# Rotary sum of queries and keys formed in PSUM by accumulated transposes instead of by an addition on VectorE

## The chip, the cores and the metric

The kernel runs on one core of a Trainium2 chip. The metric is the device time of one execution in microseconds (us); a median of several executions is compared with the median of the changed kernel. All data are fp32.

## What is computed

The input x is 4 sequences of 256 tokens with 256 features. One decoder block is applied: gated linear attention with decay, then four experts chosen by token id, then a second short attention whose sequence axis is the batch; a layer norm follows each. Only the first part is touched by the change:

```python
q = silu((x @ Wq).reshape(b, n, 16, 16)); k = silu((x @ Wk).reshape(b, n, 16, 16))
v = (x @ Wv).reshape(b, n, 16, 16)
q, k = rotate(q), rotate(k)      # concat(x1*cos - x2*sin, x1*sin + x2*cos) per head
# chunks of 128 tokens, two for a sequence:
scores = einsum('bthd,bshd->bhts', qi, ki) * D
o = einsum('bhts,bshd->bthd', scores, vi) + einsum('bthd,bhde->bthe', qi * decay_q, S)
S = lam_C * S + einsum('bshd,bshe->bhde', ki * decay_k, vi)
x = layernorm(x + groupnorm(o * sigmoid(x @ Wg1 @ Wg2)) @ Wo)
```

The rotation of a tile is a sum of two products: the tile times a cosine table, and the tile with the halves of each head swapped times a sine table.

## The kernel before

The 1024 tokens are 8 tiles of 128. The program is written by hand for each engine (TensorE, VectorE, ScalarE, GpSimd, and SyncE for the transfers); semaphores alone order the engines, and each engine runs its own list strictly in order. Attention runs in rounds: round i works on tile i in its first steps and on tiles i-1 and i-2 in its later ones. From round 7 on the rounds of the experts and of the last part are woven in; the change doesn't touch these.

TensorE's list in round i (`attention_round` in its block): `transpose_qk(i)`, four transposes of 128x128, the two of q into bank 2 and then the two of k into bank 7; `attend(i-1)` (state or scores times values); in even rounds `make_state(i/2)`, k times v for the state that the second chunk of the sequence needs, into bank 7; `proj_qkv(i+1)`; `scores(i, g)` for four groups g of four heads, in banks 3 and 4 by turns, of which group g waits until VectorE has emptied group g-2; `transpose_on(i-2)`, `turn_back(i-1)` and `project_o(i-2)`. In round 7 `transpose_h(0)` comes before the scores. In round 0 `transpose_experts` stands behind the transposes.

VectorE's list: `copy_kT(i)`; `gate_o(i-2)` and `norm_o(i-2)` (two wide operations, one reduction and a chain of eleven small ones, lines 681 to 686); in even rounds `decay_state`, two scalings of bank 7; `ln_apply`; `rope_cos(i+1)`, the cosine product for the next tile; the masks of scores 0 and 1, `rope_add(i+1)`, the masks of scores 2 and 3 (`mask_scores`, line 717); `residual1(i-2)`, which waits for `project_o`, and the statistics of the layer norm. Rounds 3 and 5 also prepare weights here.

ScalarE: `expand_q(i)` (eight copies of 32 partitions from bank 2), `silu_qk(i+1)`, which makes `qk`, `copy_v(i+1)`, `copy_oT(i-1)`. GpSimd: `sine_part(i+1)` (two products, line 284), `scale_o(i-2)` (line 292), then the layer norm's root. The cosine product goes to `rcos`, the sine product to `rsin`, the sum to `qkr`; each has two buffers used by turns, and `transpose_qk` and `make_state` read `qkr`. `transpose2`, line 1024, holds the transposes of several callers, and `project`, line 1029, the projections. A transpose is the matmul instruction in its transposing form, with the data as stationary operand and the identity as moving operand. In the profile a transpose leaves one record, any other fp32 matmul two.

Of the kernel before, what the change touches and what calls it, by code (L numbers as in the profile page):

```python
# [15 lines left out]
ALU = mybir.AluOpType  # L16
# [5 lines left out]
P = 128  # L22
B, S, D = 4, 256, 256
TILES = B * S // P
KT = D // P
# [62 lines left out]
def decoder_block(nc, x, tokens, ctx, wq, wk, wv, wo, wg1, wg2, norm_w, conv_w, fwq, fwk, fwv, fwg, router, fwout,  # L88
                  consts, out):
    stack = ExitStack()  # L90
    with stack:
        def sb(name, shape, dt=F32):
            return stack.enter_context(nc.sbuf_tensor(name, shape, dt))

        bank = [stack.enter_context(nc.psum_tensor(f"bank{i}", [P, 512], F32)) for i in range(8)]
# [3 lines left out]
        def S_(name):  # L99

            if name not in made:
                made[name] = stack.enter_context(nc.semaphore(name))
            return made[name]
# [28 lines left out]
        qk = sb("qk", [P, 2, 2 * D])  # L132
        rcos = sb("rcos", [P, 2, 2 * D])
        rsin = sb("rsin", [P, 2, 2 * D])
        qkr = sb("qkr", [P, 2, 2 * D])
        v_sb = sb("v_sb", [P, 3, H, 32])
        qx = sb("qx", [P, 2, KT, 8, P])
        kT = sb("kT", [P, 2, KT, P])
# [60 lines left out]
        ident = con[:, C_IDENT:C_IDENT + P]  # L199
# [60 lines left out]
        def _(eng):  # L260
# [13 lines left out]
            def sine_part(i):  # L274

                eng.wait_ge(S_("rope_tab"), 4 * (i % 2 + 1))
                if i >= 2:
                    eng.wait_ge(S_("roped"), i - 1)
                eng.wait_ge(S_("qk_silu"), i + 1)
                src = qk[:, i % 2, :].rearrange("p (h s d) -> p h s d", s=2, d=HD // 2)  # L280
                dst = rsin[:, i % 2, :].rearrange("p (h s d) -> p h s d", s=2, d=HD // 2)
                tab = rope_tab[:, i % 2, 1, :].rearrange("p (h s d) -> p h s d", s=2, d=HD // 2)
                for s in range(2):
                    eng.tensor_tensor(dst[:, :, s, :], src[:, :, 1 - s, :], tab[:, :, s, :], ALU.mult)\  # L284
                       .then_inc(S_("sine"), 1)
# [182 lines left out]
        def _(eng):  # L468
# [9 lines left out]
            def silu_qk(i):  # L478
                eng.wait_ge(S_("qk_made"), i + 1)
                if i >= 2:  # L480
                    eng.wait_ge(S_("roped"), i - 1)
                eng.activation(qk[:, i % 2, :], bank[0][:, :], ACT.Silu).then_inc(S_("qk_silu"), 1)  # L482

            def copy_v(i):
# [147 lines left out]
        def _(eng):  # L632
# [58 lines left out]
            def rope_cos(i):  # L691
                eng.wait_ge(S_("qk_silu"), i + 1)
                if i < 2:
                    eng.wait_ge(S_("rope_tab"), 4 * (i + 1))
                eng.tensor_tensor(rcos[:, i % 2, :], qk[:, i % 2, :], rope_tab[:, i % 2, 0, :], ALU.mult)\
                   .then_inc(S_("cosine"), 1)

            def rope_add(i):
                eng.wait_ge(S_("cosine"), i + 1)
                eng.wait_ge(S_("sine"), 2 * i + 2)  # L700
                if i >= 2:
                    eng.wait_ge(S_("qkT_made"), i - 1)
                    eng.wait_ge(S_("state_made"), i // 2)
                eng.tensor_tensor(qkr[:, i % 2, :], rcos[:, i % 2, :], rsin[:, i % 2, :], ALU.add)\
                   .then_inc(S_("roped"), 1)

            def copy_kT(i):
                eng.wait_ge(S_("kT_made"), i + 1)
                if i >= 2:
                    eng.wait_ge(S_("scores_made"), 4 * (i - 1))  # L710
                eng.tensor_copy(kT[:, i % 2, :, :], two(bank[7][:, 0:D])).then_inc(S_("kT_copied"), 1)
# [41 lines left out]
            def ln_apply(n, i, dst, xin, done):  # L753
                eng.wait_ge(S_(f"ln{n}_rstd"), 2 * i + 2)
                eng.tensor_scalar(dst, xin, agg[:, n, i, 0:1], rstd[:, n, i:i + 1], ALU.subtract, ALU.mult)\
                   .then_inc(S_(done), 1)
# [7 lines left out]
                ln_stats(0, i, x1[:, i % 2, :])  # L764

            rope_cos(0)
            rope_add(0)

            def mask_part(name, dst, src, j, experts, before, ready):

# [10 lines left out]
            def attention_round(i):  # L781
                if i < TILES:
                    copy_kT(i)
                if i == 0:

                    for n in range(E):
                        eng.wait_ge(S_("ctxT_made"), n + 1)
                        eng.tensor_copy(ctxT[:, :, n, :], bank[3 + n % 2][:, :].rearrange("p (k d) -> p k d", k=KT))\
                           .then_inc(S_("ctxT_copied"), 1)
                    make_masks(E + 2)  # L790
                if i >= TILES:
                    ln_apply(0, i - 3, h1[:, i - 3, :], x1[:, (i - 3) % 2, :], "h1_done")
                if 0 <= i - 2 < TILES:
                    gate_o(i - 2)
                    norm_o(i - 2)
                if i == MOE_START:
                    eng.wait_ge(S_("mask"), 6)
                    mask_part("hTe_vector", hTe, hT, 0, (0, VECTOR_EXPERTS_H), "z_made", "hT_copied")
                if i < TILES and i % 2 == 0:
                    decay_state(i // 2)  # L800
                if 0 <= i - 3 and i < TILES:
                    ln_apply(0, i - 3, h1[:, i - 3, :], x1[:, (i - 3) % 2, :], "h1_done")
                if i + 1 < TILES:
                    rope_cos(i + 1)
                for g in range(4):
                    if i < TILES:
                        mask_scores(i, g)
                    if i + 1 < TILES and g == 1:
                        rope_add(i + 1)
                if 0 <= i - 2 < TILES and i < TILES:  # L810
                    residual1(i - 2)
                if i == 3:

                    eng.wait_ge(S_("f_in"), 16 * 7)
                    rflat = rt[:, :, :, :].rearrange("p h e r -> p (h e) r")
                    link(eng.tensor_tensor(rdiff[:, :], rflat[:, :, 0], rflat[:, :, 1], ALU.subtract))
                    for k in range(KT):
                        link(eng.tensor_tensor(x2[:, k, :], f_w1[:, k, 128:384], rdiff[:, :], ALU.mult))
                        eng.tensor_reduce(f_w2[:, k, D:D + H], heads(x2[:, k, :]), AX.X, ALU.add)\
                           .then_inc(S_("wd"), 1)  # L820
                if i == 5:

                    for k in range(KT):
                        link(eng.tensor_reduce(wv_sum[:, k, :], heads(f_w1[:, k, 128:384]), AX.X, ALU.add))
                        eng.scalar_tensor_tensor(out=heads(f_w1[:, k, 128:384]),
                                                 in0=wv_sum[:, k, :].unsqueeze(2).to_broadcast([P, H, HD]),
                                                 scalar=-1.0 / HD, in1=heads(f_w1[:, k, 128:384]),
                                                 op0=ALU.mult, op1=ALU.add).then_inc(S_("wv_centred"), 1)
# [191 lines left out]
        def _(eng):  # L1020
            def transpose2(dst, src):

                for k in range(KT):
                    last = eng.transpose(dst[:, k * P:(k + 1) * P], src[:, k * P:(k + 1) * P], ident)  # L1024
                return last
# [9 lines left out]
            for k in range(KT):  # L1035
                last = eng.transpose(bank[2][0:HD, k * P:(k + 1) * P], w_g1[:, k, :], ident)
# [12 lines left out]
            for k in range(KT):  # L1049
                last = eng.matmul(bank[3][:, k * D:(k + 1) * D], w_g1T[:, k * P:(k + 1) * P], w_g2[:, :],  # L1050
                                  start=True, stop=True)
            last.then_inc(S_("wg_made"), 1)
            def proj_qkv(i):
# [12 lines left out]
                    eng.wait_ge(S_("gated"), i - 2)  # L1066
                project(bank[1][:, 0:D], xt, w_v[:, :, :]).then_inc(S_("v_made"), 1)

            def transpose_qk(i):
                eng.wait_ge(S_("roped"), i + 1)  # L1070
                if i:
                    eng.wait_ge(S_("q_expanded"), 8 * i)
                transpose2(bank[2], qkr[:, i % 2, 0:D]).then_inc(S_("qkT_made"), 1)
                if i:
                    eng.wait_ge(S_("kT_copied"), i)
                    eng.wait_ge(S_("state"), 2 * ((i + 1) // 2))
                transpose2(bank[7], qkr[:, i % 2, D:2 * D]).then_inc(S_("kT_made"), 1)

            def scores(i, g):
                eng.wait_ge(S_("q_expanded"), 8 * i + 8)  # L1080
# [34 lines left out]
            def make_state(b):  # L1115
                i = 2 * b
                eng.wait_ge(S_("kT_copied"), i + 1)
                eng.wait_ge(S_("v_copied"), i + 1)
                for f in range(KT):
                    last = eng.matmul(bank[7][:, f * D:(f + 1) * D], qkr[:, i % 2, D + f * P:D + (f + 1) * P],  # L1120
                                      v_sb[:, i % 3, 8 * f:8 * f + 8, :].rearrange("p h e -> p (h e)"),
                                      start=True, stop=True)
                last.then_inc(S_("state_made"), 1)

            def turn_back(i):
# [233 lines left out]
```

## Time and profile before

| | us |
|---|---|
| median of 3 runs | 255.02 |
| lowest, highest | 254.4, 258.87 |
| the profiled execution, first to last instruction | 256.0 |
| TensorE busy | 209.2 |
| VectorE busy | 176.7 |
| GpSimd busy | 114.0 |
| ScalarE busy | 81.7 |

The profiled execution is one execution of its own. Of it the span of the instructions is given, and no time around it; the span already lies 1.0 above the median of the runs. A share of busy time is an average over stages: the attention rounds take the time from about 23 to 120 us of the span, the rest belongs to experts and the last part.

### The profile page before, as it was taken

What the parts mean: (1) busy time and instruction counts of PE and PEld (TensorE: products, weight loads), DVE (VectorE), ACT (ScalarE), POOL (GpSimd) and SP (SyncE); (2) the same over time, 40 slices, a digit from 0 to 9 for tenths busy, and PEclk for the clock granted to TensorE, in tenths of its full rate; (3) what the DMA queues carried; (4) which work ended last, traced back from release to release, by engine and by line L of the source; (5) the groups of instructions that cost most, each with busy time, mean ns of one, the idle gap of its engine ahead of it and who ended that gap; (6) DMA issues with size and microseconds to landing.
All of it is one profiled execution on the core that took longest, in us unless ns stands there. A gap on an engine that the chain in (4) does not pass through costs nothing.

```text
span 256.0 us, 3809 instructions
## 1 busy us (share of the span) xinstructions
PE 209.2 (82%) x1254; PEld 146.0 (57%) x1254; DVE 176.7 (69%) x438; ACT 81.7 (32%) x219; POOL 114.0 (45%) x188
## 2 busy tenths in 40 slices
PE   3788999995987798849799989999999997842461
PEld 1367555562745364515799776686786966411340
DVE  1168848779597979793556863348769788897751
ACT  0075664452432534241100113403223234423021
POOL 9661207335161413140516352346558529656352
PEclk9999999999799999977979999999999999995555
DMA  7990000000000000000000000000000001001011
GB/s 195 339 299 5 3 0 4 0 1 0 3 1 0 3 1 0 3 0 0 3 0 3 1 0 0 3 1 0 0 3 0 0 4 40 3 0 41 0 38 45
DMA packets 7027, 6.65 MB, mean 26 GB/s; under 512 B 1232, under 2 KB 6624, under 8 KB 7008
## 3 DMA queue, kind: packets, MB, share of 16 engines
q1 hardware_dynamic: 5744, 5.33, 6.6%
q10 hardware_dynamic: 1264, 1.08, 1.4%
q8 instruction: 10, 0.16, 0.3%
q14 instruction: 9, 0.07, 0.1%
HBM read 5.36 MB, written 1.05 MB: 25 GB/s over the span
## 4 chain that ended last, share of the span: by engine, by line
PE 52%; DVE 24%; issue 9%; POOL 6%; ACT 4%; DMA 3%; ACTq 1%; DVEq 0%; POOLq 0%
PE bank L1029 19%; PE bank L1230 12%; PE bank L1087 9%; PE bank L1244 4%; PE bank L1024 3%; DMA w_qk<-in_L_attn_Wk 3%; DVE hTe L776 2%; DVE w_qk L937 2%; PE bank L1132 2%; DVE stats L749 1%; POOL rstd L301 1%; DVE newton L685 1%; DVE probs L717 1%; PE bank L1120 1%; DVE newton L684 1%
## 5 line engine op out<-in xcount | busy, mean ns | idle before, releaser
L1087 PE MATMUL bank<-qx,kT 128*128 128x512 f32 x64 | 33.7, 652 | 10.6 <-DVE probs L717 8.9
L1230 PE MATMUL bank<-hTe,ctxT 128*128 128x128 f32 x256 | 31.7, 285 | 2.6 <-issue 2.6
L1230 PEld LDWEIGHTS bank<-hTe,ctxT 128*128 128x128 f32 x256 | 31.0, 201 | 3.2 <-issue 3.1
L499 ACT ACTIVATE qx<-bank,con 32x256 f32<-32x256 f32 x64 | 26.4, 458 | 16.0 <-PE bank L1024 15.4
L1244 PE MATMUL bank<-ctxT,aTe 128*128 128x256 f32 x128 | 29.0, 379 | 0.0
L284 POOL TENSOR_TENSOR rsin<-qk,rope_tab 128x256 f32<-128x256 f32 x16 | 13.2, 845 | 34.9 <-ACT qk L482 34.9
L1029 PE MATMUL bank<-f_w,oT 128*128 128x512 f32 (+4 forms) x80 | 28.0, 496 | 0.8 <-ACT oT L552 0.7
L298 POOL TENSOR_SCALAR rstd<-agg 128x1 f32<-128x1 f32 x24 | 5.3, 222 | 49.3 <-DVE agg L751 48.5
L1087 PEld LDWEIGHTS bank<-qx,kT 128*128 128x128 f32 x64 | 11.7, 197 | 26.8 <-issue 24.5
L717 DVE TENSOR_TENSOR probs<-bank,con 128x512 f32<-128x512 f32 x32 | 21.6, 686 | 5.8 <-PE bank L1087 5.0
L1244 PEld LDWEIGHTS bank<-ctxT,aTe 128*128 128x128 f32 x128 | 23.7, 190 | 2.9
L336 POOL TENSOR_TENSOR aTe<-rcos,mask 128x256 f32<-128x256 f32 x8 | 11.9, 1493 | 25.5 <-DVE rcos L835 25.5
L1029 PEld LDWEIGHTS bank<-f_w,oT 128*128 128x128 f32 x80 | 14.4, 190 | 12.0 <-issue 5.7
L835 DVE TENSOR_TENSOR rcos<-rcos,bank 128x256 f32<-128x256 f32 x8 | 3.4, 420 | 21.7 <-ACT rcos L602 21.7
L1029 PE MATMUL bank<-w_qk,xT 128*128 128x512 f32 x32 | 17.0, 658 | 1.5 <-DMA w_qk<-in_L_attn_Wk 1.5
L301 POOL TENSOR_TENSOR rstd<-rstd,con 128x1 f32<-128x1 f32 x24 | 14.0, 582 | 2.0
L336 POOL TENSOR_TENSOR hTe<-hT,mask 128x512 f32<-128x512 f32 x8 | 13.3, 1656 | 2.6 <-ACT hT L539 2.6
L1024 PE MATMUL bank<-con,fgo 128*128 128x128 f32 x16 | 3.7, 357 | 12.8 <-POOL fgo L414 12.8
L512 ACT ACTIVATE onT<-bank 128x256 f32<-128x256 f32 x8 | 3.1, 384 | 33.8 <-PE bank L1024 33.8
L1029 PE MATMUL bank<-f_out,onT 128*128 128x256 f32 x32 | 11.7, 522 | 1.6 <-ACT onT L592 1.6
L1024 PEld LDWEIGHTS bank<-con,fgo 128*128 128x128 f32 x16 | 2.4, 179 | 15.2 <-POOL fgo L414 14.8
L1111 PE MATMUL bank<-probs,v_sb 128*32 128x128 f32 x256 | 10.8, 274 | 0.0
(128 smaller groups left out, 407.7 us busy)
## 6 DMA issues: line engine op xcount, KB each, us to landing
x_sb<-in_x SPq DMA_DIRECT2D x4, 256.0 KB, 6.8
ctx_sb<-in_ctx SPq DMA_DIRECT2D x1, 1024.0 KB, 12.3
out<-x_sb SPq DMA_DIRECT2D x8, 128.0 KB, 1.7
fgo<-in_itok_BxS ACTq DMA_DIRECT2D x1, 512.0 KB, 9.3
con<-shape_constants SPq DMA_DIRECT2D x1, 338.5 KB, 3.0
w_v<-in_L_attn_Wv SPq DMA_DIRECT2D x1, 256.0 KB, 5.5
w_qk<-in_L_attn_Wq ACTq DMA_DIRECT2D x1, 256.0 KB, 5.7
w_qk<-in_L_attn_Wk ACTq DMA_DIRECT2D x1, 256.0 KB, 7.3
```

What stands on the lines that cost most here:

```text
L284: eng.tensor_tensor(dst[:, :, s, :], src[:, :, 1 - s, :], tab[:, :, s, :], ALU.mult)\
L298: eng.tensor_scalar(rstd[:, n, i:i + 1], agg[:, n, i, 1:2], LN_EPS, None, ALU.add)\
L301: eng.tensor_tensor(rstd[:, n, i:i + 1], rstd[:, n, i:i + 1], half_neg, ALU.pow)\
L336: eng.tensor_tensor(dst[:, j % 2, experts[0]:experts[1], :, :], two(src[:, j % 2, :]).unsqueeze(1).to_broadcast([P, n, KT, P]), mask[:, ex ...
L499: eng.activation(qx[rr, i % 2, :, 2 * r + par, :], two(bank[2][rr, 0:2 * P]), ACT.Copy, scale=con[rr, C_PARITY + par:C_PARITY + par + 1]). ...
L717: eng.tensor_tensor(probs[:, i % 2, 4 * g:4 * g + 4, :], bank[3 + g % 2][:, :].rearrange("p (h n) -> p h n", h=4), causal.unsqueeze(1).to_ ...
L1024: last = eng.transpose(dst[:, k * P:(k + 1) * P], src[:, k * P:(k + 1) * P], ident)
L1029: last = eng.matmul(dst, lhsT[:, k, :], w[:, k, :], start=(k == 0), stop=(k == KT - 1))
L1087: eng.matmul(bank[3 + g % 2][:, :], kT[:, i % 2, g // 2, :], qx[:, i % 2, g // 2, 4 * (g % 2):4 * (g % 2) + 4, :].rearrange("p h n -> p (h ...
L1111: last = eng.matmul(bank[5][32 * n:32 * n + 32, g * P:(g + 1) * P], v_sb[:, i % 3, h, :], probs[:, i % 2, h, :], start=(i % 2 == 0), stop= ...
L1230: last = eng.matmul(bank[0][:, f * P:(f + 1) * P], ctxT[:, k, e, f * P:(f + 1) * P], hTe[:, j % 2, e, k, :], start=(e == 0 and k == 0), st ...
L1244: last = eng.matmul(bank[3][:, 0:D], aTe[:, j % 2, e, k, :], ctxT[:, k, e, :], start=(e == 0 and k == 0), stop=(e == E - 1 and k == KT - 1))
```

## The change

`rope_add` and the tile `qkr` are removed. The transposes of q and k go through a new function that transposes the cosine part and then the sine part into the same columns of PSUM, the second accumulating on the first. `make_state` multiplies both parts with v and accumulates. The waits of the functions that wrote or read these tiles are changed accordingly.

```diff
-        qkr = sb("qkr", [P, 2, 2 * D])
 def sine_part(i):          # GpSimd
-        eng.wait_ge(S_("roped"), i - 1)
+        eng.wait_ge(S_("kT_made"), i - 1)
+        eng.wait_ge(S_("state_made"), i // 2)
 def silu_qk(i):            # ScalarE
-        eng.wait_ge(S_("roped"), i - 1)
+        eng.wait_ge(S_("cosine"), i - 1)
+        eng.wait_ge(S_("sine"), 2 * (i - 1))
 def rope_cos(i):           # VectorE
     if i < 2:
         eng.wait_ge(S_("rope_tab"), 4 * (i + 1))
+    else:
+        eng.wait_ge(S_("kT_made"), i - 1)
+        eng.wait_ge(S_("state_made"), i // 2)
-def rope_add(i):
-    ...
-    eng.tensor_tensor(qkr[:, i % 2, :], rcos[:, i % 2, :], rsin[:, i % 2, :], ALU.add)
-    ...
 # VectorE's round
-        if i + 1 < TILES and g == 1:
-            rope_add(i + 1)
+def transpose_sum(dst, i, col):        # TensorE
+    for k in range(KT):
+        cols = slice(col + k * P, col + (k + 1) * P)
+        eng.matmul(dst[:, k * P:(k + 1) * P], rcos[:, i % 2, cols], ident, start=True, stop=False,
+                   is_transpose=True)
+        last = eng.matmul(dst[:, k * P:(k + 1) * P], rsin[:, i % 2, cols], ident, start=False, stop=True,
+                          is_transpose=True)
+    return last
 def transpose_qk(i):
-    eng.wait_ge(S_("roped"), i + 1)
+    eng.wait_ge(S_("cosine"), i + 1)
+    eng.wait_ge(S_("sine"), 2 * i + 2)
     ...
-    transpose2(bank[2], qkr[:, i % 2, 0:D]).then_inc(S_("qkT_made"), 1)
+    transpose_sum(bank[2], i, 0).then_inc(S_("qkT_made"), 1)
     ...
-    transpose2(bank[7], qkr[:, i % 2, D:2 * D]).then_inc(S_("kT_made"), 1)
+    transpose_sum(bank[7], i, D).then_inc(S_("kT_made"), 1)
 def make_state(b):
     for f in range(KT):
-        last = eng.matmul(bank[7][:, f * D:(f + 1) * D], qkr[:, i % 2, D + f * P:D + (f + 1) * P],
-                          v_sb[...], start=True, stop=True)
+        for part in (rcos, rsin):
+            last = eng.matmul(bank[7][:, f * D:(f + 1) * D], part[:, i % 2, D + f * P:D + (f + 1) * P],
+                              v_sb[...], start=(part is rcos), stop=(part is rsin))
```

## Rows read from the trace of the kernel before

**Rows 1.** The page: busy time by engine; clock granted to TensorE in 40 slices

```profile
PE 209.2 (82%) x1254; PEld 146.0 (57%) x1254; DVE 176.7 (69%) x438; ACT 81.7 (32%) x219; POOL 114.0 (45%) x188
...
PEclk9999999999799999977979999999999999995555
```

**Rows 2.** Chain that ended last, rounds 0 to 2 (start, us, what)

```profile
22.36 0.61 DVE rcos L695
22.99 0.70 DVE qkr L704
...
26.87 0.86 PE bank L1120 x4
27.74 2.58 PE bank L1029 x8
30.32 1.72 PE bank L1087 x4
32.05 1.95 PE bank L1087 x4
34.01 0.44 PE bank L1024 x4
```

**Rows 3.** Timeline, rounds 0 and 4 (start, us, engine, line; in brackets idle before)

```profile
23.74 0.66 PE L1024 MATMUL bank<-con,qkr 128*128 128x128 f32 x4 [0.38 <-DVE qkr L704]
...
78.18 1.96 PE L1087 MATMUL bank<-qx,kT 128*128 128x512 f32 x4 [1.40 <-DVE probs L717]
...
78.55 0.68 DVE L704 TENSOR_TENSOR qkr<-rcos,rsin 128x512 f32<-128x512 f32 x1
...
81.79 0.60 PE L1024 MATMUL bank<-con,qkr 128*128 128x128 f32 x4
81.99 0.42 DVE L762 TENSOR_TENSOR x<-bank,x_sb 128x256 f32<-128x256 f32 x1 [1.13 <-PE bank L1029]
...
83.01 0.40 DVE L711 COPY kT<-bank 128x256 f32<-128x256 f32 x1
```

**Rows 4.** Timeline, TensorE's waits in rounds 3, 4, 5, 6, 6 and 7

```profile
62.66 2.38 PE L1087 MATMUL bank<-qx,kT 128*128 128x512 f32 x4 [2.83 <-DVE probs L717]
...
71.35 1.13 PE L1120 MATMUL bank<-v_sb,qkr 128*128 128x256 f32 x4 [1.21 <-DVE kT L711]
...
89.94 1.96 PE L1087 MATMUL bank<-qx,kT 128*128 128x512 f32 x4 [2.04 <-DVE probs L717]
...
96.79 1.13 PE L1120 MATMUL bank<-v_sb,qkr 128*128 128x256 f32 x4 [0.76 <-DVE kT L711]
...
103.26 1.96 PE L1087 MATMUL bank<-qx,kT 128*128 128x512 f32 x4 [1.04 <-DVE probs L717]
...
114.97 3.75 PE L1087 MATMUL bank<-qx,kT 128*128 128x512 f32 x4 [1.55 <-DVE probs L717]
```

**Rows 5.** Chain that ended last: one stretch of experts' matmuls, 128 columns, accumulating

```profile
120.80 3.59 PE bank L1230 x32
```

**Rows 6.** Timeline of rounds 0 to 6: silu, products, decay of the state

```profile
30.12 0.69 DVE L695 TENSOR_TENSOR rcos<-qk,rope_tab 128x512 f32<-128x512 f32 x1 [0.60 <-ACT qk L482]
...
74.23 0.60 ACT L482 ACTIVATE qk<-bank 128x512 f32<-128x512 f32 x1 [2.79 <-PE bank L1029]
...
75.33 1.55 POOL L284 TENSOR_TENSOR rsin<-qk,rope_tab 128x256 f32<-128x256 f32 x2 [1.84 <-ACT qk L482]
...
76.22 1.21 DVE L695 TENSOR_TENSOR rcos<-qk,rope_tab 128x512 f32<-128x512 f32 x1
...
99.68 0.60 ACT L482 ACTIVATE qk<-bank 128x512 f32<-128x512 f32 x1 [2.33 <-PE bank L1029]
...
100.44 1.52 POOL L284 TENSOR_TENSOR rsin<-qk,rope_tab 128x256 f32<-128x256 f32 x2 [4.41 <-ACT qk L482]
...
101.30 1.21 DVE L695 TENSOR_TENSOR rcos<-qk,rope_tab 128x512 f32<-128x512 f32 x1
```

**Rows 7.** Windows: us, busy by engine, then granted clock (1.00 is full)

```profile
63.00:64.00 1.00, 1.00 (x3) 0.38 (x2) 0.92 (x3) 0.00 (x0) 0.00 (x0) 1.00 0.00 0
...
66.00:67.00 1.00, 1.00 (x5) 0.81 (x4) 0.00 (x0) 0.00 (x0) 0.00 (x0) 0.50 0.00 0
...
116.00:117.00 1.00, 1.00 (x3) 0.48 (x2) 0.00 (x0) 0.00 (x0) 0.00 (x0) 0.50 0.00 0
```

**Rows 8.** Timeline, VectorE's residual behind the output projection: rounds 3 and 7

```profile
67.85 0.42 DVE L762 TENSOR_TENSOR x<-bank,x_sb 128x256 f32<-128x256 f32 x1 [2.09 <-PE bank L1029]
...
120.62 0.42 DVE L762 TENSOR_TENSOR x<-bank,x_sb 128x256 f32<-128x256 f32 x1 [1.17 <-PE bank L1029]
```

More of the change, by code:

```diff
@@ L694, in rope_cos @@
                     eng.wait_ge(S_("rope_tab"), 4 * (i + 1))
+                else:
+                    eng.wait_ge(S_("kT_made"), i - 1)
+                    eng.wait_ge(S_("state_made"), i // 2)
                 eng.tensor_tensor(rcos[:, i % 2, :], qk[:, i % 2, :], rope_tab[:, i % 2, 0, :], ALU.mult)\
                    .then_inc(S_("cosine"), 1)
-            def rope_add(i):
[L699 to L705, printed above, removed]
             def copy_kT(i):
@@ L766, in _ @@
             rope_cos(0)
-            rope_add(0)
             def mask_part(name, dst, src, j, experts, before, ready):
@@ L1119, in make_state @@
                 for f in range(KT):
-                    last = eng.matmul(bank[7][:, f * D:(f + 1) * D], qkr[:, i % 2, D + f * P:D + (f + 1) * P],
-                                      v_sb[:, i % 3, 8 * f:8 * f + 8, :].rearrange("p h e -> p (h e)"),
-                                      start=True, stop=True)
+                    for part in (rcos, rsin):
+                        last = eng.matmul(bank[7][:, f * D:(f + 1) * D], part[:, i % 2, D + f * P:D + (f + 1) * P],
+                                          v_sb[:, i % 3, 8 * f:8 * f + 8, :].rearrange("p h e -> p (h e)"),
+                                          start=(part is rcos), stop=(part is rsin))
                 last.then_inc(S_("state_made"), 1)
```

## The prediction

> **What bounds the kernel now.** I read the page first: TensorE is busy for 82% of the span and VectorE for 69% [rows 1]. That says nothing about one stage, so next came the chain of work that ended last, and then the timeline of each attention round, with a look at which engine sat idle in front of what.
>
> In rounds 0 to 2 the chain is TensorE almost without a break: state, projections, scores, transposes, projections [rows 2]. Here an instruction more on TensorE is time, and one less on VectorE is none, except at the very start, where the chain goes mask, cosine, sum, transposes [rows 2].
>
> From round 3 on a round has two halves. After the residual VectorE works its long list (copy of kT, gate, norm, layer norm, cosine product, masks 0 and 1) and TensorE, done with scores 0 and 1, waits for the first mask: 2.83 us in round 3, 1.40 in round 4, 2.04 in round 5, 1.04 in round 6, 1.55 in round 7 [rows 3, 4]. Then TensorE sets the pace (scores 2 and 3, transposes, output projection) and VectorE waits 1.13 us for the projection [rows 3]. The sum over `rcos` and `rsin`, 0.68 us, lies in this second half, at 78.55, with VectorE's wait for the projection behind it [rows 3]. So in these rounds it is already hidden. The added work of TensorE, on the other hand, lies in the first half, in front of TensorE's wait.
>
> **The change part by part.**
>
> Transposes. Each tile gets eight in place of four. Four take 0.44 us in the chain, 0.11 each [rows 2]. The added ones have the same form with another data tile; what the trace of before doesn't show is a transpose that accumulates. The nearest rows are the experts' matmuls with 128 moving columns, which accumulate in runs of eight: 32 records in 3.59 us, 0.112 a record, no dearer for accumulating [rows 5]. The bounds are thus 0.11 and, if the accumulating form ran like any fp32 matmul with its two records, 0.22. I take 0.11, since the operands are those of a transpose. That adds 4 x 0.11 = 0.44 a round, half of it before ScalarE can expand q, all of it before kT can be copied.
>
> State. Two matmuls of 256 columns become four. The two take 0.86 us in the chain, four records at 0.215 [rows 2]; so +0.86 in rounds 0, 2, 4 and 6. Accumulating over two operands is what every projection does [rows 2], so I see only one price.
>
> Sum removed: 8 x 0.68 = 5.4 us of VectorE's time, of which only the first is on the path.
>
> Round 0: TensorE was idle 0.38 us for the sum, and the transposes started at 23.74, 0.78 after the cosine product's end at 22.97 [rows 2, 3]. They can start earlier by 0.38 to 0.78, less what the projections before still occupy; I take 0.55. Then +0.44 for transposes and +0.86 for the state: +0.75. Round 1: +0.44. Round 2: +0.44 + 0.86 = +1.30. No wait of TensorE of any size is in between that could take this up [rows 2], so rounds 0 to 2 give 2.5 us.
>
> Round 3: +0.44 into a wait of 2.83; kT's copy waits for VectorE's statistics rather than for the transposes: 0. In round 4 the transposes themselves lie in front of a wait of 1.21 for the kT copy [rows 4] and vanish in it; the state's 0.86 moves the projections, and with them silu, from an end at 74.83 to 75.69, just in front of the cosine product that started at 76.22 [rows 6]. Scores 0 and 1 move by 0.86 into the wait of 1.40: about 0. Round 5: +0.44 into 2.04; kT's copy started at 83.01, 0.62 behind the transposes' end at 82.39 [rows 3], so with 0.44 more it still fits: 0. Round 6: a wait of 0.76 in front of the state takes the transposes [rows 4]; the state's 0.86 goes into 1.04, and silu's end moves from 100.28 to 101.14, with the cosine product's start at 101.30 [rows 6]: about 0. Round 7: expansion of q later by 0.22, and through it TensorE's scores and ScalarE's copy of hT, on which GpSimd and VectorE wait: +0.2.
>
> The cover in rounds 4 and 6 is thin, 0.2 to 0.5 us, and there is one more thing moved there: the two sine products of GpSimd, which follow silu. In round 4 the cosine product ran beside a sine product and took 1.21 us against 0.69 in round 1 [rows 6], and the sine products and the cosine product meet again, only in another order. Bounds are a gain of 0.5 (they miss each other, 1.21 becomes 0.69) and a loss of one more such stretch, 0.5. For rounds 4 to 6 I take +0.3 together, since the order changes but the number of operations that meet does not.
>
> Waits. `sine_part`, `rope_cos` and `silu_qk` wait for events of TensorE, VectorE and GpSimd that lie a round back (transposes and state of tile i-2, products of tile i-2); behind these waits stand the same operations as before, and none ends later than silu of the tile itself. So they cost nothing, and the removed sum gives `rcos` free no later than `qkr` was.
>
> Sum: 2.5 + 0.3 + 0.2 = 3.0 us. Against the profiled execution, 256.0 becomes 259.0; its span lies 1.0 above the median and nothing in the rows says that the added work depends on that, so I add the same to the median: 255.02 + 3.0 = 258.0. What measurement of this kernel can tell from no change is about 2%, 5.1 us, and the forecast is inside it.
>
> **Clock.** TensorE's granted clock is full in most rounds, and half, 1.2 GHz, in the windows 66 to 67 and 116 to 117 [rows 1, 7], in each case after a wait for VectorE [rows 4]. It costs: from the start of scores 2 to the residual round 4 needs 81.99 - 78.18 = 3.81 us [rows 3], round 3 needs 67.85 - 62.66 = 5.19 and round 7 needs 120.62 - 114.97 = 5.65 [rows 4, 8], so 1.4 and 1.8 us. Such falls can come and go when waits move.
>
> **The rivals.**
>
> A, the clock stays up. In round 3 TensorE's wait falls from 2.83 to 2.4; with 2.04 in round 5 there was no fall [rows 1, 4]. If it stays up in round 3: 258.0 - 1.4 = 256.6; in round 7 too: 254.8. For it: the wait shrinks toward one that did no harm. Against it: it shrinks by only 0.4. By the Trainium skill ("TensorE: Matmul & The Clock Gate", Part 4) a transpose in transposing mode doesn't count as activity for the clock as other matmuls do; in round 3 only transposes are added, so by that rule the fall stays and the time is the forecast's. No row of before separates the two. The opposite, one fall more of the size of round 7's, gives 258.0 + 1.8 = 259.8.
>
> B, slower: VectorE's list gets longer in rounds 4 to 7, since the sine products come later and meet the cosine product and the small operations at a worse place. The place is the stretch from silu to the first mask. It decides once silu ends after VectorE is ready for the cosine product (76.2 in round 4, 101.3 in round 6), that is from a delay of about 0.9 to 1.4, where I reckon 0.86; then all that comes over it counts, and the stretch of 0.5 with it. If the transposes are not taken up by the kT copy's wait, the delay is 1.3: 0.4 + 0.5 in rounds 4 and 6 and 0.5 in 5 and 7, together 2.8: 258.0 + 2.8 = 260.8. The Trainium skill ("SBUF — State Buffer", "SBUF: two separate sides") has an operation of VectorE with two SBUF inputs blocked for the whole of a GpSimd operation; the 1.21 against 0.69 agrees, and this is what would make an ill-placed sine product dear.
>
> C, the accumulating transposes run at 0.22. Then eight cost 1.76 where four cost 0.44: 0.9 more in each round than reckoned, 2.7 in rounds 0 to 2; in 4 and 6 the slack is gone, 0.9 each, and in 3, 5 and 7 the kT copy comes some 0.7 late: 258.0 + 2.7 + 1.8 + 2.1 = 264.6. Against it: rows 5.
>
> D, VectorE's time counts after all: the four sums in rounds 3 to 6 would give back 0.68 each, 2.7 in all: 255.3. For it: VectorE sets the first half of each of these rounds. Against it: the sum stands in the other half, with 1.13 us of waiting behind it [rows 3].
>
> **How the numbers follow.** Forecast 0.50 (own range 256.5 to 259.5), A 0.17, one fall more 0.07, B 0.12, C 0.08, D 0.06. The range leaves out C (0.08), the lower part of A (0.04, the clock kept in more places than round 3 and 7) and an upper part of B (0.05); it takes in both bounds of the sine products, 0.5 either way, on the forecast and on its neighbours: 254.6 to 261.6. Slower by over 2% means above 260.1: C, most of B, a part of the case with one more fall: 0.22. Faster by over 2% means below 249.9, which no case reaches: 0.02. The rest, 0.76, is within 2%.
>
> **What would show it.** Transposes of `rcos` and `rsin` 0.11 us apart, 64 in all; state of eight records, 1.7 us; attention rounds 0 to 2 longer by 2.5 us at the start of round 3; TensorE's waits for the first mask shorter by 0.4 in odd rounds and by most of 0.9 in even ones, with starts of scores 2 unmoved relative to the residual before; VectorE's wait for the output projection longer. The prediction is wrong if the accumulating transposes leave gaps, if the cosine product waits for silu in rounds 4 and 6, or if granted clock differs in rounds 3, 7 or in the experts' rounds.

## The result, and the profile after

| | before | changed |
|---|---|---|
| median, us | 254.82 | 259.01 |
| lowest to highest, 4 executions each | 254.4 to 258.87 | 257.58 to 260.16 |
| ratio, 95% interval | | 1.0136 [1.007, 1.0202] |

The changed kernel is slower by 1.4%, 3.5 us by the ratio; 258.0 was forecast, range 254.6 to 261.6. Before's median is that of the three executions the forecast started from (255.02) and a fourth, 254.62. Every ratio in this document leaves out executions more than 1.5% above the fastest of the same kernel (10 of 28 of before on the chip of the first experiments), so it is not the quotient of the medians beside it. The traced execution took 257.58 us, of which 255.8 is the span: 1.8 us lie around it. The traced execution of before has a span of 256.0, so it was one of before's longer ones, near 257.8, and not a typical one. Subtracting the two spans gives -0.2 us, with the wrong sign; the sections below show why.

The page of the changed kernel, first lines (the same views as in [rows 1]):

```profile
PE 212.1 (83%) x1302; PEld 150.8 (59%) x1302; DVE 172.5 (67%) x430; ACT 81.6 (32%) x219; POOL 113.2 (44%) x188
...
PEclk9999999999999999999979999999999999996555
```

TensorE has 48 records more and 2.9 us more of busy time, VectorE 4.2 us less. By the forecast's prices TensorE should have 8 x 0.44 + 4 x 0.86 = 7.0 us more. What is missing is clock, since work at half clock is busy for longer. From residual to residual TensorE is busy for 11.09 us before and 10.11 changed in round 3, and for 10.14 and 7.99 in round 7, though 0.44 was added in each: 1.4 and 2.6 of the missing 4.1. In [rows 1] the 7 of slice 11 (round 3) and those of slices 18 and 19 (round 7) are falls that the changed kernel's execution doesn't have. The one of slice 21 it has too.

The changed kernel's first transposes and state, in the timeline (start, us, engine, line):

```profile
21.29 1.22 DVE L664 TENSOR_TENSOR mask<-mask 128x1024 f32<-128x1024 f32 x1
...
22.42 0.68 DVE L699 TENSOR_TENSOR rcos<-qk,rope_tab 128x512 f32<-128x512 f32 x1
...
23.34 0.27 PE L1065 MATMUL bank<-con,rcos 128*128 128x128 f32 x1
23.45 0.27 PE L1067 MATMUL bank<-con,rsin 128*128 128x128 f32 x1
...
23.56 0.27 PE L1065 MATMUL bank<-con,rcos 128*128 128x128 f32 x1
23.66 0.27 PE L1067 MATMUL bank<-con,rsin 128*128 128x128 f32 x1
...
26.69 0.60 PE L1124 MATMUL bank<-v_sb,rcos 128*128 128x256 f32 x2
27.12 0.59 PE L1124 MATMUL bank<-v_sb,rsin 128*128 128x256 f32 x2
```

A start every 0.11 us: the accumulating transpose costs what the plain one does, and the state's records start 0.215 apart. The first transposes start 2.05 us after the start of the mask operation at 21.29, where before it was 23.74 - 21.14 = 2.60: earlier by 0.55.

The same timeline, TensorE's waits and VectorE's residual in rounds 3 to 7, which answer to [rows 4, 8]:

```profile
56.51 0.42 DVE L757 TENSOR_TENSOR x<-bank,x_sb 128x256 f32<-128x256 f32 x1 [1.19 <-PE bank L1021]
...
65.25 1.96 PE L1090 MATMUL bank<-qx,kT 128*128 128x512 f32 x4 [2.40 <-DVE probs L712]
...
69.06 0.42 DVE L757 TENSOR_TENSOR x<-bank,x_sb 128x256 f32<-128x256 f32 x1 [1.13 <-PE bank L1021]
...
72.56 0.70 PE L1124 MATMUL bank<-v_sb,rcos 128*128 128x256 f32 x2 [0.78 <-DVE kT L706]
...
79.82 1.96 PE L1090 MATMUL bank<-qx,kT 128*128 128x512 f32 x4 [0.97 <-DVE probs L712]
...
91.59 1.96 PE L1090 MATMUL bank<-qx,kT 128*128 128x512 f32 x4 [1.61 <-DVE probs L712]
...
98.45 0.70 PE L1124 MATMUL bank<-v_sb,rcos 128*128 128x256 f32 x2 [0.32 <-DVE kT L706]
...
102.86 3.85 PE L1090 MATMUL bank<-qx,kT 128*128 128x512 f32 x8
...
116.61 1.96 PE L1090 MATMUL bank<-qx,kT 128*128 128x512 f32 x4 [2.19 <-DVE probs L712]
...
120.43 0.42 DVE L757 TENSOR_TENSOR x<-bank,x_sb 128x256 f32<-128x256 f32 x1 [1.13 <-PE bank L1021]
```

The waits ahead of scores 2 in rounds 3 and 5 and ahead of the state in rounds 4 and 6 are shorter by the transposes added in front of them, 0.44: 2.83 became 2.40, 2.04 became 1.61, 1.21 became 0.78 and 0.76 became 0.32. In round 4 the state's 0.86 takes only 0.43 from the wait ahead of scores 2, 1.40 to 0.97, because VectorE's half of the round got longer by 0.43; in round 6 the wait of 1.04 is gone. In round 7 the wait is longer, 2.19 for 1.55, because scores 0 and 1 in front of it ran at full clock. Scores 2 in rounds 3 and 7 ran at full clock too: 1.96 us where [rows 4] have 2.38 and 3.75.

Where the addition's time went shows in VectorE's list in round 4, before and then changed:

```profile
79.31 0.69 DVE L717 TENSOR_TENSOR probs<-bank,con 128x512 f32<-128x512 f32 x1
80.17 0.69 DVE L717 TENSOR_TENSOR probs<-bank,con 128x512 f32<-128x512 f32 x1 [0.17 <-PE bank L1087]
```

```profile
80.95 0.69 DVE L712 TENSOR_TENSOR probs<-bank,con 128x512 f32<-128x512 f32 x1 [0.68 <-PE bank L1090]
81.81 0.69 DVE L712 TENSOR_TENSOR probs<-bank,con 128x512 f32<-128x512 f32 x1 [0.17 <-PE bank L1090]
83.64 0.42 DVE L757 TENSOR_TENSOR x<-bank,x_sb 128x256 f32<-128x256 f32 x1 [1.13 <-PE bank L1021]
```

The mask of scores 2 starts 1.13 us after scores 2 in both (78.18 and 79.31, 79.82 and 80.95). Before, the addition stood in this time and VectorE did not wait; now it waits 0.68 for the scores, the whole length of the addition. The wait for the output projection is 1.13 in both.

To compare kernels whose rounds start at different times I read two kinds of stretches out of every trace: from the start of the last mask operation before tile 0's cosine product to the first residual (rounds 0 to 2), and from residual to residual (rounds 3 to 7). In us:

| trace | rounds 0 to 2 | 3 | 4 | 5 | 6 | 7 |
|---|---|---|---|---|---|---|
| before | 32.79 | 13.92 | 14.14 | 11.76 | 13.32 | 13.55 |
| changed | 35.22 | 12.55 | 14.58 | 11.77 | 13.16 | 11.86 |
| changed, again | 35.22 | 12.56 | 14.57 | 11.76 | 13.17 | 11.85 |
| state only | 34.51 | 13.98 | 14.57 | 11.76 | 13.16 | 11.72 |
| transposes only | 33.49 | 14.15 | 14.44 | 11.76 | 13.33 | 11.85 |
| cosine alone | 32.45 | 14.06 | 14.45 | 11.75 | 13.33 | 11.72 |
| addition kept | 35.22 | 13.94 | 14.57 | 11.77 | 13.17 | 11.85 |
| filled in round 3, matmuls | 32.78 | 12.55 | 14.14 | 11.77 | 13.33 | 13.10 |
| filled in round 3, transposes | 32.79 | 12.55 | 14.14 | 11.77 | 13.34 | 11.72 |
| filled in rounds 3 to 7 | 32.79 | 12.57 | 14.14 | 11.77 | 13.33 | 11.73 |
| the same, again | 32.78 | 12.55 | 14.14 | 11.77 | 13.34 | 11.71 |
| filled in rounds 3 to 8 | 32.78 | 12.55 | 13.62 | 11.77 | 12.80 | 11.72 |
| changed, filled | 35.21 | 12.57 | 14.57 | 11.77 | 13.16 | 11.85 |

Round 3 takes 12.55 or about 14, round 7 about 11.8 or over 13: the longer ones are those in which the granted clock fell to half, 1.2 GHz in place of 2.4. Without falls before is 32.79, 12.55, 14.14, 11.77, 13.33, 11.72, and the changed kernel adds 2.43 + 0 + 0.43 + 0 - 0.17 + 0.14 = 2.8 us. The rest of the span, from the last residual on, is 135.4 in both traces.

The fall of round 7 in the trace of before began earlier than the 116 to 117 of [rows 7]: scores 0 and 1 already took 2.70 us, where the changed kernel has 1.98, behind a wait for ScalarE and ahead of the wait for VectorE's mask. The granted clock, third number from the end, was down by 112:

```profile
110.72 2.70 PE L1087 MATMUL bank<-qx,kT 128*128 128x512 f32 x4 [1.67 <-ACT qx L499]
```

```profile
112.00:113.00 1.00, 1.00 (x2) 0.00 (x0) 1.00 (x2) 0.00 (x0) 0.97 (x1) 0.50 0.00 0
```

### The profile page after: what moved, and what is told of

It reads as the page before. It is cut to its first block, busy times and chain, and to the rows that moved or that the text cites. A ratio compares the mean times of both kernels' runs of the same rounds, so it can differ in the third digit from the quotient of the medians.

```text
span 255.8 us, 3896 instructions
## 1 busy us (share of the span) xinstructions
PE 212.1 (83%) x1302; PEld 150.8 (59%) x1302; DVE 172.5 (67%) x430; ACT 81.6 (32%) x219; POOL 113.2 (44%) x188
## 4 chain that ended last, share of the span: by engine, by line
PE 54%; DVE 22%; issue 9%; POOL 6%; ACT 4%; DMA 3%; ACTq 1%; POOLq 0%; DVEq 0%
PE bank L1021 20%; PE bank L1234 12%; PE bank L1090 9%; PE bank L1248 4%; DMA w_qk<-in_L_attn_Wk 3%; PE bank L1016 2%; PE bank L1124 2%; DVE w_qk L929 2%; DVE hTe L770 2%; DVE stats L744 1%; POOL rstd L301 1%; PE bank L1136 1%; DVE newton L685 1%; DVE newton L686 1%; DVE probs L712 1%
## 5 line engine op out<-in xcount | busy, mean ns | idle before, releaser
L1090 PE MATMUL bank<-qx,kT 128*128 128x512 f32 x64 | 30.8, 603 | 8.9 <-DVE probs L712 7.2
L1090 PEld LDWEIGHTS bank<-qx,kT 128*128 128x128 f32 x64 | 11.1, 189 | 23.9 <-issue 21.6
L750 DVE TENSOR_SCALAR h<-x,agg,rstd 128x256 f32<-128x256 f32 x16 | 8.9, 564 | 3.9 <-POOL rstd L301 3.9
## 6 DMA issues: line engine op xcount, KB each, us to landing
x_sb<-in_x SPq DMA_DIRECT2D x4, 256.0 KB, 6.8
w_v<-in_L_attn_Wv SPq DMA_DIRECT2D x1, 256.0 KB, 5.3
w_qk<-in_L_attn_Wq ACTq DMA_DIRECT2D x1, 256.0 KB, 5.8
w_qk<-in_L_attn_Wk ACTq DMA_DIRECT2D x1, 256.0 KB, 7.3
```

The costliest lines, as they stand in the source:

```text
L1090: eng.matmul(bank[3 + g % 2][:, :], kT[:, i % 2, g // 2, :], qx[:, i % 2, g // 2, 4 * (g % 2):4 * (g % 2) + 4, :].rearrange("p h n -> p (h ...
```

## The experiments

The first four ran on one chip beside 28 executions of the kernel before (median 257.2; a 29th, of 713 us, is left out), the next four on another beside 33 (256.9), the last four on a third beside 17 (257.26). These medians of before are 2.1 to 2.4 us above the 254.82 of the four executions above.

### The state from both parts, nothing else

```diff
-        last = eng.matmul(bank[7][...], qkr[...], v_sb[...], start=True, stop=True)
+        for part in (rcos, rsin):
+            last = eng.matmul(bank[7][...], part[...], v_sb[...],
+                              start=(part is rcos), stop=(part is rsin))
```

The waits that keep `rcos` and `rsin` from being overwritten too early are added as in the change, here and in the next kernel.

> The kernel before, with one part of the change: the state is made from the cosine and the sine part (four matmuls in place of two in rounds 0, 2, 4, 6); the addition on VectorE and the transposes of its sum stay. My theory (the path is TensorE in rounds 0 to 2, VectorE up to the first mask from round 3 on): +0.86 in rounds 0 and 2, nearly nothing in rounds 4 and 6 (up to +0.4 in all), so +1.7 to +2.1 us. Rival (every instruction added to TensorE is time, because it is the busiest engine): 4 x 0.86 = +3.4 us. Rival (clock): falls of the clock come and go and hide it; then the start of the residual in rounds 1 to 3 still shows +1.7.

Median 257.75, ratio 1.006 [1.0017, 1.0103]. Rounds 0 to 2 are longer by 1.72, twice 0.86 as expected. Round 4 is longer by 0.43, round 6 shorter by 0.16. So 2.0 us of 3.4 of added TensorE work is time, within the 1.7 to 2.1 expected.

### The transposes by pairs, nothing else

```diff
 def transpose_qk(i):
-    transpose2(bank[2], qkr[:, i % 2, 0:D])
+    transpose_sum(bank[2], i, 0)
-    transpose2(bank[7], qkr[:, i % 2, D:2 * D])
+    transpose_sum(bank[7], i, D)
```

> The kernel before, with the other part: q and k are transposed by pairs that accumulate the cosine and the sine part; the addition on VectorE stays, but only the state reads its result. My theory: +0.44 in each of rounds 0 to 2, less the 0.55 by which the first transposes start earlier, nothing in rounds 3 to 6, +0.1 in round 7: +0.8 to +1.0 us. Rival (all added TensorE time counts): 8 x 0.44 - 0.55 = +3.0 us. Rival (accumulating transposes cost 0.22 each): over 4 us.

Median 256.97, ratio 1.0012 [0.9977, 1.0046]. Rounds 0 to 2 are longer by 0.70 (expected 3 x 0.44 - 0.55 = 0.77), round 7 by 0.13 (expected 0.1), round 4 by 0.30 where nothing was expected. Together with the state alone that is 1.72 + 0.70 = 2.42 for rounds 0 to 2, and the changed kernel has 2.43: there the parts add up.

### The addition removed with none of its price

```diff
-        eng.matmul(dst[...], rcos[:, i % 2, cols], ident, start=True, stop=False, is_transpose=True)
-        last = eng.matmul(dst[...], rsin[:, i % 2, cols], ident, start=False, stop=True, is_transpose=True)
+        last = eng.matmul(dst[...], rcos[:, i % 2, cols], ident, start=True, stop=True, is_transpose=True)
 # make_state
-        for part in (rcos, rsin):
+        for part in (rcos,):
```

> The changed kernel without the sine part on TensorE: transposes and state read the cosine part alone, so the rotation leaves out its sine term; the sine products are still made, and all waits are those of the changed kernel. This is the removal of the addition with none of its price. My theory: the addition lay on the path only in front of round 0, so -0.5 to -0.6 us against the kernel before. Rival (VectorE bounds rounds 3 to 6, the addition counts there): -0.55 - 4 x 0.68 = -3.3 us.

Six executions, median 255.47, ratio 0.9897 [0.9827, 0.9966], wide since single executions here went from 252.77 to 258.57. The interval leaves out the 0.5 to 0.6 us of the theory and takes in the 3.3 of the rival, so these executions alone would speak for the rival; the rounds of the trace do not: -0.34 in rounds 0 to 2, nothing in 3, 5, 6 and 7 beyond the clock, +0.3 in round 4. VectorE's four additions in rounds 3 to 6 were worth nothing. Of the 0.55 of the earlier start 0.2 were lost again, to a wait that I had not seen. In its timeline:

```profile
22.98 0.60 PE L1065 MATMUL bank<-con,rcos 128*128 128x128 f32 x4
23.18 0.39 ACT L519 ACTIVATE gate<-bank 128x256 f32<-128x256 f32 x1 [0.48 <-PE bank L1021]
...
23.71 1.06 PE L1155 MATMUL bank<-con,ctx_sb 128*128 128x128 f32 x8
```

`transpose_experts` waits for ScalarE's last gate, which ends at 23.57, while four transposes at 0.11, from 22.98 on, were through at 23.42. In the changed kernel eight transposes fill that time.

### The changed kernel once more

> The changed kernel once more, with more rounds, beside the parts on one chip. My theory: +3.0 us from instructions (2.6 in rounds 0 to 2, 0.4 behind), plus or minus what the clock does in single executions (a fall in round 3 costs 1.4, one in round 7 costs 1.8): the ratio between 1.008 and 1.018. If clock falls were rarer in the changed kernel as a rule, its best runs would be less than 2.5 us above the best runs of before.

Twelve executions, median 257.66, ratio 1.0018 [0.9985, 1.005], below the 1.008 expected. Every stretch of its trace is that of the first trace within 0.01 us, so the instructions cost the same; what differs is before. The clock says how. The mean granted clock of the executions beside each other is 0.9432 for the changed kernel, all twelve between 0.939 and 0.947, and 0.9346 for before, with most executions at 0.938, 0.932, 0.930 or below. At like clock the kernels differ as the instructions do: the executions of before at 0.943 to 0.945 have 253.95, 254.41, 254.90, 255.13 and 255.95, median 254.90; those of the changed kernel at 0.944 and 0.945 have 256.86, 257.54 and 257.78, median 257.54: 2.6 us more. At 0.938 to 0.940 four of each have medians of 256.4 and 258.9, 2.5 apart. This is not so at 0.942, with 257.25 and 257.42 before and 257.87 changed, so a like mean clock does not mean like falls in every execution.

### The addition kept on VectorE

Seven of the eight additions are put back; the first tile's is not.

```diff
+def rope_add(i):        # as before, reads rcos and rsin; nobody reads qkr
+    eng.tensor_tensor(qkr[:, i % 2, :], rcos[:, i % 2, :], rsin[:, i % 2, :], ALU.add)
 ...
                         mask_scores(i, g)
+                    if i + 1 < TILES and g == 1:
+                        rope_add(i + 1)
```

> The changed kernel with the addition put back on VectorE at its old place in rounds 0 to 6, writing a tile that nobody reads. My theory (the addition lies in VectorE's wait for TensorE): the residual of each round starts where it does in the changed kernel, within 0.1 us, and the time is that of the changed kernel, 257.7 plus or minus 0.7. Rival (the addition counts in rounds 3 to 6): +2.7 us, above 260.

All stretches are those of the changed kernel within 0.01 us, but for round 3, which had a fall of the clock. The addition sits in VectorE's wait for scores 2:

```profile
64.47 0.67 DVE L707 TENSOR_TENSOR qkr<-rcos,rsin 128x512 f32<-128x512 f32 x1
65.56 0.69 DVE L720 TENSOR_TENSOR probs<-bank,con 128x512 f32<-128x512 f32 x1 [0.42 <-PE bank L1100]
```

The median, 259.04, ratio 1.0074 [1.004, 1.0108], is above the 257.0 to 258.4 that I expected. It had a mean clock of 0.9397 against 0.9432. No instruction moved; whether kept additions make falls likelier or the executions happened to have more of them, these runs do not tell. The chips differ too.

### Idle matmuls in the wait of round 3

```diff
+def keep_busy(i, n):
+    if n:
+        eng.wait_ge(S_("ln0_sum"), i - 2)
+    for _ in range(n):
+        eng.matmul(bank[6][:, 0:D], ident, w_g[:, 0, :], start=True, stop=True)
 # round 3, behind scores 1: keep_busy(3, 4)
```

The wait in `keep_busy` makes sure that VectorE has read the last residual out of bank 6, which the idle matmuls overwrite.

> The kernel before with four idle fp32 matmuls of 256 columns (1.7 us, result unused) in TensorE's wait for the first mask of round 3, which shrinks from 2.8 to about 1.1 us. Theory (the fall of the clock in round 3 comes from this wait): no fall there, round 3 takes 12.55 us from residual to residual in place of 13.9, the mean granted clock rises by 0.006 and the median falls by about 1.4 us. Rival (the fall hangs on something else, such as the phase of the execution): round 3 still takes 13.9, or falls elsewhere, and the median stays.

Ratio 0.9973 [0.9933, 1.0012], median 256.16 beside 256.9, mean clock 0.9397 beside 0.9356. The trace has no fall in round 3 (12.55), one in round 7. The median fell by 0.7 where 1.4 was expected, and the interval takes in no change.

### Idle transposes in the same wait

```diff
-        eng.matmul(bank[6][:, 0:D], ident, w_g[:, 0, :], start=True, stop=True)
+        eng.transpose(bank[6][:, 0:P], ident, ident)
 # sixteen of them
```

> The same with sixteen idle transposes of 128 columns in the same place, also 1.7 us. By the rule of the Trainium skill (TensorE: Matmul & The Clock Gate, Part 4) a transpose does not count as activity as other matmuls do. Then the clock falls in round 3 as in the kernel before and the median is that of before. If transposes keep the clock as well as matmuls, the median is that of the kernel filled with matmuls, 1.4 us less.

Ratio 0.9965 [0.9924, 1.0005], median 256.15, mean clock 0.9403, no fall in round 3. Median, mean clock and round 3 are those of the matmuls: here fp32 transposes were as good as matmuls for the clock, and the rule of the Trainium skill ("TensorE: Matmul & The Clock Gate", Part 4) that the expectation names does not show. Against before neither of the two is separated from no change by its interval. What both traces show is the missing fall in round 3, which five of the seven traces without idle work have.

### Idle matmuls in the waits of rounds 3 to 7

The edit is that of the first filled kernel, with a count for each round.

> The kernel before with idle matmuls of 256 columns in TensorE's waits of rounds 3 to 7 (four, two, three, one, two behind scores 1, and three ahead of the scores of round 7), each 0.43 us and shorter in sum than the wait. Theory (what separates the two kernels in single executions is how often the clock falls in these waits): falls in rounds 3 and 7 go, mean granted clock about 0.945, median near the best executions of before, 254 to 254.5, so about 2.5 us below before and 3 below the changed kernel. Rival: the fillers delay scores or take slack, and the time stays or rises.

Eleven executions, median 254.27, ratio 0.9907 [0.9873, 0.9941], mean clock 0.9481. The same window of round 3 in the kernel before and in this one (us, busy by engine, then granted clock, the third number from the end):

```profile
64.00:70.00 6.00, 6.00 (x80) 4.67 (x78) 3.19 (x8) 2.26 (x6) 0.86 (x2) 0.72 0.01 3
```

```profile
64.00:70.00 6.00, 4.81 (x80) 3.58 (x78) 4.53 (x12) 3.52 (x9) 2.15 (x5) 1.00 0.01 3
```

The rounds' stretches equal those of before wherever before had no fall, so the idle work costs nothing.

### The changed kernel filled, and the kernel before filled again

> The changed kernel with idle matmuls in its waits of rounds 3, 4, 5 and 7 (four, one, three, three behind scores 1, two ahead of the scores of round 7), to be set beside the kernel before with such matmuls. Theory (instructions cost 3.0 us, and the clock gives part of it back since the added work shortens TensorE's waits): with the waits filled in both, the clock is alike, about 0.947, and the full price shows: 254.3 + 3.0 = 257.3, so this is hardly faster than the changed kernel itself (257.7). Rival (the change's price is itself only about 1 us): 255.3.

> The kernel before with its waits of rounds 3 to 7 filled, once more, on the chip of the filled changed kernel. Theory: 254.3, 0.9 to 1.2 per cent below before, 3.0 below the filled changed kernel.

On one chip: 257.06 (256.05 to 257.81, twelve executions, ratio 1.0013 [0.998, 1.0045]) and 253.44 (252.82 to 255.19, six executions, ratio 0.9897 [0.9849, 0.9945]). With the mean clock held up in both (0.946 before, 0.950 changed), the change costs 3.6 us, more than the 2.8 of the rounds and in line with the 3.0 expected as far as six and twelve executions can say. The rival, a price of about 1 us, is out. The filled changed kernel is only 0.6 below the unfilled one's 257.66 on another chip; that its waits are shorter from the start would explain it, but the two were not run beside each other.

### One more wait filled

```diff
                 if i == TILES:
                     transpose_h(j + 1)
+                    keep_busy(i, 4)
                 expert_up(j)
```

> The same with four more idle matmuls in TensorE's wait ahead of the second up-projection of the experts (round 8), behind which the clock fell in most traces and cost 1.85 us. Theory: no fall between 126 and 135 us, mean clock 0.954, 252.4 to 252.8, which is 1.6 below the kernel filled in rounds 3 to 7 alone. Rival: the fall moves to another place and the time stays at 254.3.

Median 252.93, ratio 0.9875 [0.9829, 0.9922], mean clock 0.9573. Windows of the kernel filled in rounds 3 to 7, and of this one, with the clock as the third number from the end:

```profile
126.00:135.00 9.00, 9.00 (x51) 8.51 (x50) 5.11 (x17) 0.77 (x2) 3.80 (x3) 0.81 0.01 2
```

```profile
126.00:135.00 9.00, 8.90 (x62) 8.15 (x61) 5.64 (x16) 0.77 (x2) 5.25 (x7) 1.00 0.01 2
```

The fall there is gone in this trace, and in that of the next kernel. That alone shows little, since three of the twelve traces without this filling (state only, transposes only, changed and filled) don't have it either; the mean clocks of the executions, 0.957 and 0.955 beside 0.946 for the kernel filled in rounds 3 to 7, say more. The median gains 0.5 over the kernel filled in fewer waits, where 1.6 was expected from always against never; the two intervals overlap. In this trace rounds 4 and 6 are 13.62 and 12.80 with the instructions of all the others that have 14.14 and 13.33. The timeline of round 4 shows the cosine product undisturbed, 0.69 us, where [rows 6] have 1.21, and the pair of sine products stretched in its place, 2.16 us for 1.55 (the second of them 1.48 us, where it is 0.88 in the kernel filled in rounds 3 to 7):

```profile
74.26 0.69 DVE L695 TENSOR_TENSOR rcos<-qk,rope_tab 128x512 f32<-128x512 f32 x1
```

```profile
73.37 2.16 POOL L284 TENSOR_TENSOR rsin<-qk,rope_tab 128x256 f32<-128x256 f32 x2 [1.84 <-ACT qk L482]
```

In both kernels the cosine product starts 0.9 us after the first sine product. So it was not the order or the distance of the starts that differed, but which of the two operations held up the other.

### The first sum ahead of the last mask

```diff
             for t in range(2, TILES):
                 copy_xT(t)
-                make_masks(t - 2)
+                if t < TILES - 1:
+                    make_masks(t - 2)
 ...
             rope_cos(0)
             rope_add(0)
+            make_masks(TILES - 3)
```

> The same with the cosine product and the sum of tile 0 ahead of VectorE's last mask operation. It takes the one gain that the change had, the earlier start of the first transposes, without added work. Theory: another 0.5 us less, 252.0 to 252.3; the first transposes start as soon as the gate projections are through. Rival: the mask operation, now later, delays the copy of kT in round 0 and nothing is gained.

Median 252.9, ratio 0.9864 [0.9822, 0.9906]: no different from the kernel before it. The first transposes follow the gate projections at once, but the wait for ScalarE's gate takes nearly half of it back, as with the cosine alone. Measured from VectorE's last copy of x ahead of them, the transposes start 0.54 earlier than in the kernel before, `transpose_experts` 0.31 and the first residual 0.27, where 0.5 was expected:

```profile
23.82 0.60 PE L1026 MATMUL bank<-con,qkr 128*128 128x128 f32 x4
24.02 0.38 ACT L518 ACTIVATE gate<-bank 128x256 f32<-128x256 f32 x1 [0.48 <-PE bank L1031]
...
24.54 1.06 PE L1155 MATMUL bank<-con,ctx_sb 128*128 128x128 f32 x8
```

Round 4 took 13.62 here too, but round 6 13.33. The expected 252.0 to 252.3 was missed, and so gains of this size are below what six executions can tell. These last kernels are the fastest of the study, 1.2 to 1.4% below before, and they keep the addition on VectorE.

## Why the prediction was right

**Sum.** 3.0 us of instructions was forecast, 2.8 is in the traces. Rounds 0 to 2: forecast +2.5, measured +2.43, and the parts one by one: state 1.72, transposes with the earlier start 0.70. Earlier start 0.55, as taken. Rounds 3 and 5: 0, measured 0. Rounds 4 to 6 together: +0.3, measured +0.26, though not as small losses but as +0.43 in round 4 and -0.17 in round 6; that they nearly cancel was luck. Round 7: +0.2, measured +0.14.

**Signs.** Most came as told: transposes 0.11 apart, the state at 0.215 a record, rounds 0 to 2 longer by 2.4. Three did not. VectorE's wait for the output projection did not grow, 1.13 in both; what grew was its wait for scores 2, by the addition's 0.68. So the addition was hidden in another wait than the prediction says, and in round 4 it filled that wait with nothing to spare. The start of scores 2 in round 4 moved by 0.43 relative to the residual before. And the granted clock differed in rounds 3 and 7, which the prediction itself names as a sign of being wrong.

**The number.** The 3.0 us of instructions are borne out by the traces. That the medians agree with it so well, 3.5 by the ratio, is in part luck. The difference of medians is 4.2 with the first four executions of each kernel, 0.4 with 12 beside 28, 2.1 for the kernel with the addition kept, whose stretches are the changed kernel's, and 3.6 with both filled. With the later median of before, 257.2, the same sum would have given 260.2 for a kernel that measured 257.66 there.

**Rival C**, accumulating transposes at 0.22: refuted, 0.11 apart.

**Rival D**, the addition counts in rounds 3 to 6: refuted twice in the traces, by the kernel that keeps it (same stretches) and by the one that drops it without a price (no gain in rounds 3 to 6).

**Rival B**, sine products at a worse place: its mechanism is real and its price was smaller. In round 4 VectorE's `ln_apply`, 0.40 before, took 0.84 beside a sine product in the changed kernel:

```profile
77.07 1.45 POOL L284 TENSOR_TENSOR rsin<-qk,rope_tab 128x256 f32<-128x256 f32 x2 [2.38 <-ACT qk L483]
77.11 0.84 DVE L750 TENSOR_SCALAR h<-x,agg,rstd 128x256 f32<-128x256 f32 x1
...
77.87 1.21 DVE L699 TENSOR_TENSOR rcos<-qk,rope_tab 128x512 f32<-128x512 f32 x1
```

That is one more stretch, the upper bound of 0.5; in round 6 the cosine product ran in 0.68 where it had taken 1.21, and VectorE was ahead so far that it waited 0.28 for the first scores, so TensorE set the pace there. The state is not the only thing that sets this off: the kernels with transposes only and with the cosine alone lost 0.3 in round 4 with silu starting 6.38 after the residual as before, and the kernel filled in rounds 3 to 8 gained 0.5 with nothing moved. What decides which operation is held up was not found. It is not chance from one execution to the next as far as two traces each can tell: the changed kernel and the kernel filled in rounds 3 to 7 were traced twice, and rounds 4 and 6 came out the same within 0.01 us.

**Rival A**, the clock: it had 0.17 and holds the step that was mis-sized. I wrote that nothing in the rows says that the added work depends on the traced execution. It does: that execution had falls in rounds 3 and 7, worth 3.2 us, which is about what it lay above the median (its span and the 1.8 around it make 257.8, 2.8 above 255.02, and not the 1.0 by the span alone), and the changed kernel has such falls less often. At like clock the change costs 2.5 to 2.6, with the waits filled in both 3.6 us; unfilled on one chip, 28 executions against 12, the medians differ by only 0.4. That filled waits raise the mean clock of before from about 0.935 to 0.948 and bring 0.9%, with no stretch of the instructions changed, shows that falls come from TensorE's waits. These need not be waits for VectorE, as the prediction has it: in round 7 of before the fall began behind a wait of 1.67 for ScalarE. That the change's own added work does the same to a lesser degree follows from the clocks (0.943 against 0.935) and its shorter waits; in round 3 the clock fell in all three traces with a wait of 2.8 (before, state only, cosine alone), in two of four with a wait of 2.4 (transposes only and addition kept, not the two of the changed kernel) and in none of seven with a wait of 1.1 or less, so its length counts but doesn't decide alone. Why the four first executions of before were so much better than most later ones stays open.

## What to carry to other kernels

Before moving an operation to the busiest engine, find on which side of that engine's wait it lies: here the addition was in VectorE's slack in all rounds but the first, and its replacement in TensorE's path for three rounds of eight. Compare traces round by round, from one event to the same event, since two single spans can differ by clock more than by the change and even in sign. Where TensorE waits for microseconds between bursts, idle matmuls in the wait can be worth more than a rearrangement: 0.9 to 1.2% here.

## What the runs showed of the hardware

An fp32 transpose that accumulates on another starts 0.11 us after it, like a plain one. Sixteen idle fp32 transposes kept the clock as four idle fp32 matmuls did, mean 0.940 in both, 0.936 without. With the same instructions in rounds 4 and 6, a round took 13.62 or 14.14 and 12.80 or 13.33 in different kernels, by which of two overlapping operations of VectorE and GpSimd was held up: cosine product 0.69 and second sine product 1.48 us, or 1.21 and 0.88. Executions of the kernel before spread by 5 us on each chip, by mean granted clock: on the second chip those at 0.944 had a median of 254.6, at 0.938 of 256.3, at 0.932 of 257.1.
